# First gather loop of a graph network: the weighted rows laid out with the 16 slots innermost

## What is computed

```python
q = (feats @ Wq + bq).reshape(n, H, D)      # n = 3125, H = 4, D = 16
k = (feats @ Wk + bk).reshape(n, H, D)
v = (feats @ Wv + bv).reshape(n, H, D)
score = jnp.sum(k[src] * q[dst], axis=-1)
score = jnp.exp(jnp.clip(score / SCALE, -5.0, 5.0))
wv = jax.ops.segment_sum(v[src] * score[..., None], dst, num_segments=n)
z = jax.ops.segment_sum(score, dst, num_segments=n)
wv = wv / (z[..., None] + 1.0)
```

## Time and profile before

| | us |
|---|---|
| median of three runs | 2864.03 |
| lowest and highest | 2863.81, 2866.63 |
| the profiled execution | 2857.82 |
| its span in the profile | 2856.0 |

### The profile page before, as it was taken

The page is one execution under the profiler, slowest core; times in us unless marked ns, Lnnn a source line. Parts: engine busy times, 40 slices in busy tenths (PEclk is TensorE's granted clock), DMA queues, the critical chain, the costliest instruction groups (busy, mean ns, idle before and its releaser), DMA issues.

```text
span 2856.0 us, 29389 instructions
## 1 busy us (share of the span) xinstructions
PE 1404.1 (49%) x4582; PEld 607.2 (21%) x4583; DVE 2067.5 (72%) x3682; ACT 1215.1 (43%) x3258; POOL 1806.8 (63%) x1831
## 2 busy tenths in 40 slices
PE   2224555555544545334544444444434422388994
PEld 1101111111111111112311111111111100187552
DVE  6857777878856666677677888888767877844376
ACT  0013344344333333443355665666545545531222
POOL 3467777777777777773477777767777777203012
PEclk9996667666655666666555555555555555569997
DMA  5232222222222222221122222222222211108430
GB/s 139 58 80 59 57 58 62 57 58 60 52 62 59 61 63 62 63 63 28 49 59 59 59 60 63 58 56 66 50 59 59 56 30 30 48 1 292 146 112 7
DMA packets 124408, 187.02 MB, mean 65 GB/s; under 512 B 63129, under 2 KB 78958, under 8 KB 124186
## 3 DMA queue, kind: packets, MB, share of 16 engines
q0 software_dynamic: 57776, 89.59, 14.7%
q1 hardware_dynamic: 47598, 70.70, 7.9%
q10 hardware_dynamic: 18973, 26.03, 2.6%
HBM read 146.36 MB, written 39.84 MB: 65 GB/s over the span
## 4 chain that ended last, share of the span: by engine, by line
issue 15%; PE 12%; POOL 12%; DVE 7%; ACT 6%; DMA 3%; DVEq 2%; POOLq 2%; ACTq 0%
POOL arena L584 12%; ACT arena L1379 3%; PE mm L761 3%; DVE red L2136 3%; PE hist L991 2%; DMA arena<-b_tab,lin 2%; PE tp L991 2%; PE mm L913 2%; PE l L991 1%; PE l L1088 1%; PE tp L745 1%; DMA arena<-kv_tab,rec 1%; DMA rec<-rec_tab,win 1%; DVE arena L2159 1%; POOLq L677 1%
## 5 line engine op out<-in xcount | busy, mean ns | idle before, releaser
L584 POOL DMA_INDIRECT arena<-b_tab,lin x815 | 809.1, 993 | 290.2 <-issue 266.5
L584 POOL DMA_INDIRECT arena<-kv_tab,rec x815 | 810.6, 995 | 261.5 <-issue 236.9
L821 PE MATMUL l<-arena,identB 128*128 128x512 bf16 x996 | 389.7, 557 | 525.3 <-DVE arena L2012 516.5
L1379 ACT ACTIVATE arena<-arena,lin 128x64 f32<-128x64 f32 x1984 | 479.5, 333 | 0.0
L2136 DVE TENSOR_REDUCE red<-arena 128x128 f32<-128x2048 f32 x189 | 459.5, 2485 | 13.6 <-issue 12.8
L913 PE MATMUL mm<-Wshared,eaT 48*128 48x512 f32 x248 | 234.2, 1097 | 400.3 <-ACT eaT L1373 390.6
L2012 DVE TENSOR_SCALAR arena<-arena,digit 128x512 bf16<-128x512 int16 x744 | 257.3, 414 | 57.6 <-PE l L821 43.1
L843 PE MATMUL hist<-arena,oh_lo 125*128 125x225 bf16 x400 | 170.6, 583 | 235.5 <-DVE arena L1983 235.5
L821 PEld LDWEIGHTS l<-arena,identB 128*128 128x128 bf16 x996 | 114.7, 127 | 794.8 <-DVE arena L2012 618.7
L1376 ACT ACTIVATE arena<-arena 128x1024 f32<-128x1024 f32 x62 | 65.5, 1057 | 433.0 <-DVE arena L2159 433.0
L1298 ACT ACTIVATE arena<-T,digit,negdigit 128x512 bf16<-128x512 f32 x248 | 188.4, 806 | 8.6
(11 more groups left out here) (402 smaller groups left out, 2434.8 us busy)
## 6 DMA issues: line engine op xcount, KB each, us to landing
arena<-at_tab SPq DMA_DIRECT2D x50, 800.0 KB, 4.7
at_tab<-T ACTq DMA_DIRECT2D x25, 800.0 KB, 3.5
arena<-kv_tab,rec POOLq DMA_INDIRECT x815
arena<-b_tab,lin POOLq DMA_INDIRECT x815, 2.5
at_pack<-arena SPq DMA_DIRECT2D x25, 256.0 KB
T<-at_pack SPq DMA_DIRECT2D x25, 256.0 KB, 2.8
lin_tab<-lin ACTq DMA_DIRECT2D x62, 64.0 KB, 1.6
lin<-lin_tab SPq DMA_DIRECT2D x62, 56.0 KB, 1.8
```

Of the source, the lines that this page charges most:

```text
L584: return pool.indirect_dma_start(dst, None, table, offs(ap=index, axis=0))
L821: last = pe.matmul(l3[:, 0, :], identB[:], hot[:, j], start=False, stop=True, skip_group_check=True)
L1379: last = act.activation(dst[:, s], hh[u][:, s, 0:C], ACT.Identity, bias=bias[:, s:s + 1])
```

## The change

`weighted[u]` keeps its place and its size, but the columns are now outermost and the 16 slots innermost. The three accesses to it follow: L2019 and L2021 write it through a rearranged view, and in the order in which they wrote it before, so that two products after each other now land 16 words (64 bytes) apart; the reduction L2026 takes it as it lies. No instruction is added, removed or moved.

```diff
-        weighted = [at(6208, P, SLOTS, C + HEADS), at(21754, P, SLOTS, C + HEADS)]
+        weighted = [at(6208, P, C + HEADS, SLOTS), at(21754, P, C + HEADS, SLOTS)]
...
-                e_ = weighted[u][:, :, C:C + HEADS]
+                e_ = weighted[u][:, C:C + HEADS].rearrange("p h s -> p s h")
                 tt(e_, expd[u][:], bc(masks[u], HEADS), ALU.mult)
                 d()
-                tt(weighted[u][:, :, 0:C].rearrange("p s (h c) -> p s h c", h=HEADS),
+                tt(weighted[u][:, 0:C].rearrange("p (h c) s -> p s h c", h=HEADS),
                    G[u][:, :, C:2 * C].rearrange("p s (h c) -> p s h c", h=HEADS),
                    e_.unsqueeze(3).to_broadcast([P, SLOTS, HEADS, HD]), ALU.mult)
                 end_step(u)
                 d().then_inc(LOOP0.free, 1)
-                red_(red[:, 0:C + HEADS], weighted[u].rearrange("p s c -> p c s"), X_AXIS, ALU.add)
+                red_(red[:, 0:C + HEADS], weighted[u], X_AXIS, ALU.add)
```

## The result

The changed kernel takes 2896.13 us (median of 5 runs, 2893.43 to 2897.18) against 2864.03 (5 runs, 2863.81 to 2866.63): a ratio of 1.0109, 95% interval 1.0096 to 1.0122. It is slower by 32.1 us. The forecast was 2902.1 us, in the range 2852 to 2915.

What follows compares the result with a forecast made beforehand. The first gather loop was taken as paced by POOL's gathers, in its middle and last two steps by VectorE. Terms +13.9, +5.0, +19.3 and -0.1 make +38.1 us: 2864.0 to 2902.1, range 2852 to 2915.

Steps and rivals of the forecast that it cites:

- second stretch: First gather loop, 514.9 to 790.5 us, 16 steps paced by VectorE: +12.3 on POOL, less 7.3 of waits, +5.0 us.
- first and third stretch: First gather loop, 182 to 514.9 and 790.5 to 1296 us, paced by POOL: +13.9 and +19.3 us.
- The reduction: L2026 reads 16 neighbours per sum: from 2101 to 1287 ns, 0.81 us saved a step, nothing for POOL.
- The product: L2021 writes each value 64 bytes from the last: from 1.225 to 1.99 us, 0.77 more a step.
- the first reading of the record copies: From L1610's copy: a scattered write slows its stream like a strided read, so L2021 pays 1.79 ns a value.
- the second, which gave 2855: Other reading of L1610's copy: the limit is on lines written by both streams together, so L2021 pays nothing.
- The held gather: A gather begun inside L2021 ends 0.8 us after it, so it and POOL's stream grow by 0.77 us.
- POOL's waits: Five gaps before gathers, 1.43 to 3.04 us, waiting for a buffer VectorE frees after L2021; 7.3 us in all, swallowed.
- (a): Rival: L2021's scattered write is free; only VectorE-paced parts gain, 8.9 us, giving 2855; chance 0.18.
- (d): Rival: the gather begun in L2021 isn't held longer by a longer product; POOL's 43 steps unchanged, 2863; chance 0.06.
- (b, c): Rivals on L2021's price: partial, say 0.3 us, 2873, chance 0.08; dearer, 1.07 us, 2920, chance 0.07.
- (e): Rival: the reduction L2026 stays at 2.1 us while the product grows 0.77; 47 us more, 2911; chance 0.04.

Runs made afterwards that it cites:

- e2_write_only: Kernel before with only the product's write scattered as in the change, the reduction still strided (sums wrong): 3344.49 us against 3334.60, ratio 1.0041.
- c0_changed_again: The changed kernel itself, timed again on a chip with unexplained idle stretches: 3316.41 us against 3334.94 for the kernel before, ratio 0.9939.
- e1_reduce_only: Kernel before with only the reduction reading 16 neighbours per sum, the write unchanged (sums wrong): 3338.04 us against 3334.60, ratio 1.0043; retimed 3346.93.
- g0_before_again: The kernel before, unchanged, profiled a second time on a chip like the first; the kernel before took 2858.82 and 2858.93 us there.
- g1_quads: Kernel before with `weighted` in four groups of 4 slots, product values landing 16 bytes apart: 2899.22 us, 40.3 more than the kernel before.

## Why the prediction was right

The mechanism held at each step, and the sizes were off by up to a quarter (+6.3 us for +5.0 in the second stretch).

*The bound.* POOL paced the first and third stretch and VectorE the second, and the loss came as was worked out, through a POOL whose instructions were not touched. VectorE's own step is unchanged (16.8 and 17.3 us, 16.85 and 17.34 before; -0.04 forecast).

*The reduction.* 1286 ns, 1287 forecast.

*The product.* 1942 ns, 1.99 us forecast: a scattered write costs 1.74 ns a value, not the 1.79 of the scattered read, so it pays 0.72 and not 0.77. The choice of the first reading of the record copies is borne out in its number (e2_write_only), the second, which gave 2855, is refuted. L2019, left out of the sum at up to 0.05, costs those 0.05.

*The held gather.* Forecast 0.77 more, since the gather would still end 0.81 after the product. It ends 0.70 to 0.71 after a product that writes scattered (after, c0_changed_again, e2_write_only) and 0.81 to 0.82 after one that doesn't (e1_reduce_only). The gather starts 0.06 us earlier in the product (0.86 us after its start, not 0.92), and the product is 0.72 longer, so the gather is 0.72 + 0.06 - 0.11 = 0.67 us longer; 0.65 is measured (means of 1.783 and 1.129 us). This is the mis-sized term: the tail of the hold was taken as a constant and isn't quite one.

*The stretches.* The heads of the steps (the start of L1989) moved by +11.6 us over the first stretch (13.9 forecast; 18 x 0.66 = 11.9), by +6.3 over the second (5.0) and by +16.3 over the third (19.3; 25 x 0.66 = 16.5). The second is the only one that came out dearer. There the five gathers that followed POOL's waits were not held before and now are, as POOL arrives late enough to be caught in L2021: 11 x 0.66 + 5 x 0.85 = 11.5 us, just the excess that the trace gives to L2021; less 8.1 of shortened waits (7.3 in the five of the earlier trace rows, and 0.8 in a sixth gap, of 1.12 us at 530.2), plus 2.1 in gathers caught in other products, which I hadn't counted, that is 5.5 of the 6.3. The other 0.7 is lateness that POOL already had at the start of the stretch (+12.35 us for the last gather of the step at 515 us, +11.65 for its L1989), where VectorE hadn't waited for it. Beside the earlier trace rows, the timeline of DVE at the end of the changed loop:

```profile
1354.57 1.90 DVE L2021 TENSOR_TENSOR arena<-arena 128x1024 f32<-128x1024 f32 x1
1356.71 1.29 DVE L2026 TENSOR_REDUCE red<-arena 128x68 f32<-128x1088 f32 x1 [0.25 <-issue]
1358.19 0.23 DVE L2029 TENSOR_TENSOR arena<-arena,red 128x68 f32 x1 [0.19 <-issue]
...
1361.53 1.83 DVE L2071 TENSOR_TENSOR arena<-arena,small 128x1600 f32<-128x1600 f32 x1 [1.66 <-DMA at_pack<-arena]
```

L2029 is 34.0 us later than before and L2071 34.5: the 1.21 us of waiting have become 1.66, so that the faster last reduction is worth nothing, as was said. The loop thus costs 34.1 to 34.5 us where the sum had 38.1.

*The rest.* Behind the loop the two profiles drift apart by another 3 us: +34.5 at L2071, +35.9 at the first gather of the second loop, +37.6 at the end. No line there was changed. The kernel before, profiled twice, differs from itself by 1.1 us in its span (2856.0 and 2857.1) and by 1.7 at the last L1989 of the loop, and its executions lie between 2857.8 (the profiled one) and 2866.6 us, so part of it may be chance; the cause wasn't followed further. That the forecast for the profiled execution, 2895.9, met the measured 2895.4 is therefore partly luck: a sum 4 too high and 3.5 us that nothing in it stood for. The median came out 6.0 us below its forecast: 0.5 from that sum, and 5.5 because the first profile lay 6.2 us below its median and the second only 0.7.

*The rivals.* The free write (a) fell with 1942 ns. The hold of constant length (d), which gave 2863, fell with 1.73 to 1.82 us in all 61 gathers begun in L2021. The partial and dearer prices (b, c) fell with the product, and (e) with 1286 ns. The halves' totals would have given each part its own time; on the chips where they ran they couldn't. So the way from the held gathers to the time rests on the two pairs of profiles without stops (before and after, g0_before_again and g1_quads), and no run there takes the hold away to see the time come back.

## What to carry to other kernels

A layout that turns a strided read into a run of neighbours turns the write into a strided one; before it is counted as a gain, price both, and try pairs, which gave 1220 and 1288 ns here where either pure layout pays 1.9 to 2.1 us on one side. Equal totals on one engine aren't an equal kernel: of a product and a reduction, only the product with two SBUF inputs held the gathers, so 0.72 us moved from the one to the other cost about 0.65 us a step on another engine, where that engine set the pace. Look for each instruction of the pacing engine that starts inside the instruction that you lengthen.

## What the runs showed of the hardware

- A gather issued while VectorE multiplies two operands from SBUF ends 0.81 to 0.82 us after the product (0.69 to 0.72 when the product writes scattered, 0.76 to 0.78 when it reads scattered). With one operand from PSUM it isn't held at all: 0.95 us, in 91 of 91 gathers of three kernels. A gather begun 0.34 us before the product isn't held either (0.95 us).
- Single fp32 values 16 bytes apart are written as slowly as 64 bytes apart (2006 and 1942 ns for 1024). Runs of two written, and values read 8 bytes apart, go at the full 1.04 ns a value.
- The same program took 2864 us where it was first timed, 2859 on a chip like that, and 3335 on two others, with durations of the long instructions equal within 1% and idle stretches of several microseconds for which the profile shows no cause. On one of those the change reads as 0.6% faster, where it is 1.1% slower on the first chip. A ratio measured on one kind of chip doesn't carry over to the other.
